# A graph layer's self-loop product: one small product per tile, or all of them at the start and a sum on VectorE

## The chip, the cores and the metric

The kernel runs on one core of a Trainium2 chip. Its time is device microseconds of one execution; given is the median of the runs, and less is better. A core has TensorE (matrix products into PSUM, eight banks of 128 x 512 float32), VectorE, ScalarE, GpSimd, and SyncE, which here only issues DMAs. Each engine works through its own program in order and waits for the others by semaphores.

## The reference

A graph of 3125 nodes and 103125 edges, sorted by destination, 128 features. First comes a relational layer with four bases and eight edge types, a self-loop product, a feed-forward product and two layer norms; then two attention layers (TransformerConv, two heads) and a last layer norm. The part that matters here:

```python
Hb = einsum('ni,bio->bno', h, V)              # four bases
m = sum_b w_comp[etype][:, b] * Hb[b][src]    # a message per edge
agg = segment_sum(m * norm, dst)
hn = relu(agg + h @ loop_w + bias)            # the self-loop product and its bias
y = hn @ ffn_w.T + ffn_b + h
y = layernorm(y) * ln_g + ln_b
x1 = layernorm(h + y)
```

Here h is the input x. All arithmetic is float32.

## The kernel before, in words

The 3125 nodes are 25 tiles of 125. For each tile of destination nodes the message stage gathers up to 64 edges per node by indirect DMA, builds for pairs of nodes a one-hot matrix of the sources' low digits (`low_onehot`) and a matrix of the edge weights by high digit and basis (`high_weights`), and multiplies them on TensorE (`pair_products`, L857). ScalarE copies the results out of PSUM (`evacuate`, L962). TensorE multiplies them with the rows of x (`sums`, L869: 25 products for each of the two halves of a tile), and ScalarE copies the result out as `aggT` (L981). The same matrices give edge counts, whose logarithm becomes a bias of 3125 columns per node for the attention layers (L972, L880, L989, L755); SyncE stores these in four pieces per tile (L639). A step of GpSimd, `coefs` (L574 to L577), makes the weights of a later tile's edges per basis.

The work is pipelined over steps. In the step t of the loop, w = t - 3 is the tile whose pairs are multiplied, u = t - 4 the tile whose sums are completed and activated, z = t - 5 the tile whose norms are finished. `pipeline_loop` writes the first and the last steps out and runs the others in a hardware loop, two per turn. The order within a step is written out by hand for each engine.

What becomes of one tile u within its step:
- TensorE multiplies the loop weights with the tile's turned features (`loopw`, `xt`, L935) and the four basis matrices with aggT (L937), all accumulated in one PSUM region `acc`. The middle piece of the next tile's first-half sums follows (`sums(w, 0, 1)`, nine products), then a wait for `h_ok` and `x_t_ok`, then the ffn product (L945), and then the last piece of these sums.
- ScalarE, between the first and the second half of its `counts_out`, applies Relu with the loop bias to acc and writes hT (L1041), and behind it copies the turned x1 of tile z over that tile's part of xT (L1043).
- VectorE adds the row x + ffn_b to the ffn product's result at the beginning of the next step (`first`, L769), and takes its moments. Its step consists mainly of `build_hot` (L734, L736, L739; eight per tile, four of them for the next tile and standing last in the step) and of `slot_kinds` before the last of these.

xT [128, 3125] holds the turned features. In the step of tile w = 0 TensorE turns all of x in groups of four tiles (`turn_inputs`, seven groups, two PSUM banks in turn), and ScalarE copies each group into xT (`turned_out`). Later each tile's part is overwritten with the turned x1, which the attention layers read. As the loop product needs the old features at an address that a register gives, ScalarE copies them first into the small tile `xT_tile` (L1002).

Of the kernel before, what the change touches and what calls it, by code (L numbers as in the profile page):

```python
# [71 lines left out]
def is_int(t):  # L72
    return isinstance(t, int)
# [116 lines left out]
def turn_inputs(nc, pe, m, turned_ps, turned_ok, at=0):  # L190

    x, eye, ps = m["x"], m["eye"], m["ps"][at:at + 2]
    pe.wait_ge(m["x_in"], 16)
    for n, (g, k) in enumerate(TURNS):
        if n >= 2:
            pe.wait_ge(turned_ok, n - 1)
        for i in range(k):
            last = nc.tensor.transpose(ps[n % 2][0:128, i * R:(i + 1) * R], x[:, g + i, :], eye[0:R, 0:R])
        last.then_inc(turned_ps, 1)


def turn_ffn(nc, pe, m, turned_ps, to):
# [256 lines left out]
def message(nc, a, m):  # L459
# [5 lines left out]
    with ctx:  # L465
        def sb(name, shape, dt):
            return ctx.enter_context(nc.sbuf_tensor(name, shape, dt))

        def sem(name):
            return ctx.enter_context(nc.semaphore(name))  # L470

        x, xT, eye, ones, iota, ids, ps = (m[k] for k in ("x", "xT", "eye", "ones", "iota", "ids", "ps"))
        V_b, comp, firsts, loopw, lcol = m["V"], m["comp"], m["firsts"], m["loop_w"], m["loop_bias_col"]
        gain, shift, ffnT, ffnb = m["ln_g"], m["ln_b"], m["ffnT"], m["ffn_b_rows"]
        SPLIT = 64
        SIDE = (SPLIT, R - SPLIT)
# [20 lines left out]
        CT = sb("countsT", [R, T, R], BF16)  # L497
        eye16 = sb("eye16", [128, 128], BF16)
        aggT = sb("aggT", [D, BASES, R], F32)
        xt = sb("xT_tile", [128, R], F32)  # L500
        lns = [sb(f"ln{i}", [R, RUN * R], F32) for i in range(2)]
        bias = [sb(f"bias{i}", [128, RUN * R], F32) for i in range(2)]
        tiny = sb("tiny", [128, 1], F32)
# [15 lines left out]
        psC = psM[:, :].bitcast(BF16).rearrange("p (h n) -> p h n", n=128)  # L519
        acc, psY, psX = psM[:, 256:256 + R], psM[0:R, 0:D], psM[:, 128:128 + R]  # L520
        (const, s2, slot_ok, gps, codes_ok, codes_ps, codesT_ok, hot, built, pairs_ok, evac_ok, agg_ok, aggT_ok,
         ctA_ok, ctB_ok, c_ps, ln_ok, bias_ok, xt_ok, m_ps, h_ok, y_ps, y_ok, x_ok, x_ps, x_t_ok, asked1, rooted1,
         asked2, rooted2, nrm1, nrm2, lifted, s3, kinds_ok, blank_ok, turned_ps, turned_ok, first_v, first_ok, digits_ps, digitsT_ok) = (
            sem("m_" + n) for n in (
                "const", "s2", "slot_ok", "pool", "codes_ok", "codes_ps", "codesT_ok", "hot", "built",
                "pairs_ok", "evac_ok", "agg_ok", "aggT_ok", "ctA_ok", "ctB_ok", "c_ps", "ln_ok", "bias_ok", "xt_ok", "m_ps",
                "h_ok", "y_ps", "y_ok", "x_ok", "x_ps", "x_t_ok", "asked1", "rooted1", "asked2", "rooted2",
                "norms1", "norms2", "lifted", "s3", "kinds_ok", "blank_ok", "turned_ps", "turned_ok",
                "first_v", "first_ok", "digits_ps", "digitsT_ok"))
        row_ok, row_in = m["m_row_ok"], [m["row_in0"], m["row_in1"]]  # L530
        near_in, kind_in = [sem("slot_ends_in0"), sem("slot_ends_in1")], [sem("slot_kinds_in0"), sem("slot_kinds_in1")]
        out_ok = [sem("bias_out0"), sem("bias_out1")]
# [123 lines left out]
        def _(v):  # L656
# [52 lines left out]
            def first_coefs():  # L709

                then = Steps(v, first_v)
                to = codes[0]
                v.wait_ge(m["comp_in"], 16)
                v.wait_ge(kinds_ok, 1)
                for b in range(BASES - FIRST_ON_V, BASES):
                    c = comp[:, :].rearrange("p (r b) -> p b r", b=BASES)[:, b, :].unsqueeze(2).to_broadcast([128, RELS, SLOTS])
                    then(V.tensor_tensor(part_v[:, :, :], kinds[:, :, :], c, ALU.mult))
                    then(V.tensor_tensor(part_v[:, 0:4, :], part_v[:, 0:4, :], part_v[:, 4:8, :], ALU.add))
                    then(V.tensor_tensor(part_v[:, 0:2, :], part_v[:, 0:2, :], part_v[:, 2:4, :], ALU.add))
                    last = V.tensor_tensor(to[:, b, :, :], twice(part_v[:, 0, :]), twice(part_v[:, 1, :]), ALU.add)  # L720
                    if b < BASES - 1:
                        then(last)
                last.then_inc(first_ok, 1)
# [57 lines left out]
            def third(z, par):  # L781

                v.wait_ge(rooted2, z + 1)
                if not is_int(z) or z >= 2:
# [2 lines left out]
                V.tensor_scalar(xnew[par][:, :], yb[par][:, :], means[1][par][:, 0:1], roots[1][par][:, :],  # L787
                                ALU.subtract, ALU.mult).then_inc(x_ok, 1)

            def step(t, par):  # L790
                w, u, z = t - 3, t - 4, t - 5
                for k in range(UNITS):
                    if k == 0 and inside(z):
                        first(z, 1 - par)
                    if k == 2 and inside(z):
                        second(z, 1 - par)
                    if k == 4 and inside(z):
                        third(z, 1 - par)
                    if k == 4 and inside(u):
                        bias_row(u, 3)  # L800
                    if k == 1 and inside(t) and (not is_int(t) or t >= EARLY):
                        search(nc, v, m, t, par)
                    if k == 2 and is_int(t) and t == 1:
                        for s in range(EARLY):
                            search_row(s, s)
                    if k == 2 and inside(t - 1) and (not is_int(t) or t > EARLY):
                        search_row(t - 1, 1 - par)
                    if k == UNITS - 1 and inside(t - 1) and (not is_int(t) or t > 2):
                        slot_kinds(t - 1, 1 - par)
                    if k < UNITS - AHEAD and inside(w):  # L810
                        build_hot(w, 1 - par, k + AHEAD)
                    if k >= UNITS - AHEAD and inside(w + 1):
                        build_hot(w + 1, par, k + AHEAD - UNITS)
                    if k == 2 and inside(u):
                        bias_row(u, 0)
                    if k == 3 and inside(u):
                        bias_row(u, 1)
                        bias_row(u, 2)
                    if k == UNITS - 1 and is_int(t) and t <= 2 and inside(t - 1):
                        slot_kinds(t - 1, 1 - par)  # L820
                    if k == UNITS - 1 and is_int(t) and t == 1:
                        first_coefs()
            pipeline_loop(v, step, AFTER, LEAD)

        @block.tensor
        def _(pe):
# [61 lines left out]
            def step(t, par):  # L888
# [2 lines left out]
                    pair_products(w, 0)  # L891
                if w == 0:
                    pe.wait_ge(codesT_ok, 1)
                    turn_inputs(nc, pe, m, turned_ps, turned_ok, 6)
                    pe.wait_ge(turned_ok, len(TURNS))
                if inside(z):
                    pe.wait_ge(y_ok, z + 1)
                if u == 0:
# [31 lines left out]
                    nc.tensor.transpose(psX, xnew[1 - par][:, :], eye[0:R, 0:R]).then_inc(x_ps, 1)  # L930
                if inside(u):
                    read(u, 3)
                    pe.wait_ge(xt_ok, u + 1)
                    pe.wait_ge(aggT_ok, u * 2 + 2)
                    nc.tensor.matmul(acc, loopw[:, :], xt[:, :], start=True, stop=False)  # L935
                    for b in range(BASES):
                        last = nc.tensor.matmul(acc, V_b[:, b, :], aggT[:, b, :], start=False, stop=(b == BASES - 1))  # L937
                    last.then_inc(m_ps, 1)
                if inside(w):
                    sums(w, 0, 1)  # L940
# [10 lines left out]
        def _(act):  # L951
# [40 lines left out]
            def step(t, par):  # L992
# [3 lines left out]
                if inside(w):  # L996
                    evacuate(w, 0)
                if is_int(w) and w == 0:
                    turned_out(nc, act, m, turned_ps, turned_ok, 6)
                if inside(u):  # L1000
                    logs(u, 0)
                    nc.scalar.copy(xt[:, :], xT[:, bass.ds(u * R, R)]).then_inc(xt_ok, 1)  # L1002
                    logs(u, 1)
                    logs(u, 2)
                if inside(w + 1):
# [27 lines left out]
                if inside(z):  # L1033
                    act.wait_ge(x_ps, z + 1)
                if inside(u):
                    act.wait_ge(m_ps, u + 1)
                    if is_int(u) and u == 0:
                        act.wait_ge(m["w_in"], W_IN)
                    if not is_int(u) or u >= 1:
                        act.wait_ge(y_ps, u)  # L1040
                    nc.scalar.activation(hT[:, :], acc, ACT.Relu, bias=lcol[:, :]).then_inc(h_ok, 1)  # L1041
                if inside(z):
                    nc.scalar.copy(xT[:, bass.ds(z * R, R)], psX).then_inc(x_t_ok, 1)  # L1043
                if inside(w):
# [5 lines left out]
def message_any(nc, a, m):  # L1050
# [4 lines left out]
    with ctx:  # L1055
# [25 lines left out]
        names = ("e_in", "iota_ok", "dve", "at_ok", "settled", "g_in", "stored", "m_in", "summed", "xt_ok", "ln_ok", "bias_out")  # L1081
        z = {n: sem(n) for n in names}
        cw = widths()
        SUMS = BLOCKS + 2
# [35 lines left out]
        @block.scalar  # L1120
        def _(act):
            with act.Fori(0, T) as t:

                act.wait_ge(z["dve"], 1 + t * CHAIN)
                nc.scalar.copy(xt[:, :], xT[:, bass.ds(t * R, R)]).then_inc(z["xt_ok"], 1)
                act.wait_ge(z["summed"], (t + 1) * SUMS)
                for j in range(CH):
                    last = nc.scalar.activation(lns[:, CW * j:CW * j + cw[j]], ps[j][0:R, 0:cw[j]], ACT.Ln, bias=tiny[0:R, :])
                last.then_inc(z["ln_ok"], 1)

        @block.tensor
        def _(pe):
            pe.wait_ge(z["e_in"], 32)
            with pe.Fori(0, T) as t:

                pe.wait_ge(z["dve"], 1 + t * CHAIN)
                pe.wait_ge(z["xt_ok"], t + 1)
# [648 lines left out]
```

## Time and profile before

| what | value |
|---|---|
| median of 3 runs | 1972.24 us (1970.37 to 1975.23) |
| the profiled execution's own time | 1973.57 us |
| its span | 1971.7 us |
| TensorE busy | 1898.3 us, 96% |
| VectorE busy | 1448.8 us, 73% |
| ScalarE busy | 1281.9 us, 65% |
| GpSimd busy | 671.4 us, 34% |

The profile records one execution. An engine's busy time counts its own work, not waits, nor register and semaphore instructions. The span starts with the first recorded instruction; the execution's own time holds what lies around it as well. The message stage ends at about 1056 us, the two attention layers fill the rest. The message stage's profile is a repeating pattern with a period of one tile.

### The profile page before, as it was taken

What the parts mean: (1) busy time and instruction counts of PE and PEld (TensorE: products, weight loads), DVE (VectorE), ACT (ScalarE), POOL (GpSimd) and SP (SyncE); (2) the same over time, 40 slices, a digit from 0 to 9 for tenths busy, and PEclk for the clock granted to TensorE, in tenths of its full rate; (3) what the DMA queues carried; (4) which work ended last, traced back from release to release, by engine and by line L of the source; (5) the groups of instructions that cost most, each with busy time, mean ns of one, the idle gap of its engine ahead of it and who ended that gap; (6) DMA issues with size and microseconds to landing.
All of it is one profiled execution on the core that took longest, in us unless ns stands there. A gap on an engine that the chain in (4) does not pass through costs nothing. (4 is left out here: it accounts for less than half of the span.)

```text
span 1971.7 us, 53479 instructions
## 1 busy us (share of the span) xinstructions
PE 1898.3 (96%) x19165; PEld 1645.7 (83%) x19165; DVE 1448.8 (73%) x4127; ACT 1281.9 (65%) x2289; POOL 671.4 (34%) x802
## 2 busy tenths in 40 slices
PE   1899999999999999999998999999999999999998
PEld 1789999999999999999995788888887788888887
DVE  5888878887888788878744777676663777777775
ACT  0757766776677767776764666666665666666665
POOL 3676676667666765676400000000000000000000
PEclk9999999999999999999998999999999999999999
DMA  3012111211121111111103222222211233222230
GB/s 84 8 47 73 41 41 45 75 41 41 48 72 41 41 54 67 40 41 52 61 35 129 103 100 97 80 83 97 97 65 66 101 107 106 99 92 92 103 105 11
DMA packets 43019, 137.00 MB, mean 69 GB/s; under 512 B 9191, under 2 KB 24360, under 8 KB 36485
## 3 DMA queue, kind: packets, MB, share of 16 engines
q1 hardware_dynamic: 38484, 128.24, 18.1%
q0 software_dynamic: 4400, 6.80, 1.5%
q8 instruction: 104, 1.70, 0.4%
q14 instruction: 31, 0.25, 0.0%
HBM read 91.83 MB, written 43.20 MB: 68 GB/s over the span
## 5 line engine op out<-in xcount | busy, mean ns | idle before, releaser
L869 PE MATMUL ps<-matrixT,x_rows 125*128 125x256 f32 (+1 forms) x2500 | 563.5, 377 | 0.1
L869 PEld LDWEIGHTS ps<-matrixT,x_rows 125*128 125x128 f32 x2500 | 461.4, 190 | 48.4 <-issue 0.2
L1729 DVE CUSTOM_DVE_ANT_0 scores_l<-ps,bias_rows_l 125x500 f32<-125x500 f32 (+1 forms) x700 | 390.0, 619 | 29.9 <-issue 28.9
L962 ACT COPY matrixT<-ps 125x500 f32<-125x500 f32 (+2 forms) x800 | 381.6, 653 | 38.9 <-PE ps L857 38.9
L857 PE MATMUL ps<-high_weights,low_onehot 64*125 64x125 f32 x6300 | 363.9, 273 | 8.6 <-DVE high_weights L739 8.6
L857 PEld LDWEIGHTS ps<-high_weights,low_onehot 64*125 64x125 f32 x6300 | 354.1, 187 | 21.6 <-issue 15.8
L1630 ACT ACTIVATE scores_l<-scores_l,neg_max_l 125x1500 f32<-125x1500 f32 x200 | 317.3, 1600 | 7.2 <-DVE neg_max_l L1750 7.2
L1518 PEld LDWEIGHTS ps<-weightsT_l,values_l 125*64 125x64 f32 x5000 | 267.9, 136 | 36.4 <-issue 34.1
L1559 PE MATMUL ps<-eye,scores_l 125*125 125x125 f32 x2500 | 295.2, 275 | 0.0
L1559 PEld LDWEIGHTS ps<-eye,scores_l 125*125 125x125 f32 x2500 | 281.1, 189 | 10.1 <-issue 9.5
L1541 PE MATMUL ps<-kT_l,q_tile_l 64*125 64x500 f32 (+1 forms) x1400 | 287.2, 547 | 1.7 <-issue 1.6
L1518 PE MATMUL ps<-weightsT_l,values_l 125*64 125x125 f32 x5000 | 279.7, 270 | 1.6 <-ACT hT L1658 1.6
L1638 ACT COPY weightsT_l<-ps 125x500 f32<-125x500 f32 x400 | 220.6, 578 | 91.8 <-PE ps L1559 86.9
L736 DVE TENSOR_TENSOR low_onehot<-own_low,digitsT 128x1000 f32<-128x1000 f32 x200 | 280.2, 1401 | 0.0
L1737 DVE COPY weightsT_l<-ps 125x500 f32<-125x500 f32 x200 | 135.0, 677 | 159.6 <-PE ps L1559 159.4
L1541 PEld LDWEIGHTS ps<-kT_l,q_tile_l 64*125 64x125 f32 x1400 | 144.0, 183 | 112.4 <-issue 77.5
L739 DVE TENSOR_TENSOR high_weights<-high_weights,edge_weightsT 128x800 f32<-128x800 f32 x200 | 222.4, 1112 | 0.0
L574 POOL TENSOR_TENSOR coef_parts<-kinds,comp 128x512 f32<-128x512 f32 x97 | 119.4, 1231 | 234.9 <-DVE digits L703 230.6
L989 ACT ACTIVATE ln<-ps,tiny 125x1000 f32<-125x1000 bf16 x100 | 95.5, 955 | 128.2 <-DVE bias L755 87.7
L1472 POOL COPY q_tile_l<-qT_l 128x125 f32 (+1 forms) x52 | 15.3, 293 | 436.7 <-PE ps L1541 403.0
L972 ACT CAST countsT<-matrixT 125x512 bf16<-125x512 f32 (+1 forms) x200 | 162.0, 949 | 0.0
L734 DVE TENSOR_TENSOR high_weights<-iota,digitsT 128x200 f32<-128x200 f32 x200 | 79.2, 396 | 99.6 <-PE ps L857 93.0
(152 smaller groups left out, 1605.1 us busy)
## 6 DMA issues: line engine op xcount, KB each, us to landing
bias_rows_l<-bias SPq DMA_DIRECT2D x50, 1562.5 KB, 6.5
bias<-bias SPq DMA_DIRECT2D x75, 500.0 KB
x_rows<-in_x SPq DMA_DIRECT2D x1, 1562.5 KB
bias<-bias SPq DMA_DIRECT2D x25, 62.5 KB
x<-x_rows SPq DMA_DIRECT2D x25, 62.5 KB
x_rows_l<-x SPq DMA_DIRECT2D x25, 62.5 KB
out<-rows_l SPq DMA_DIRECT2D x25, 62.5 KB
dst_int<-in_dst SPq DMA_DIRECT2D x1, 402.8 KB
```

What stands on the lines that cost most here:

```text
L736: V.tensor_tensor(L[:, at, 0:p, :], own_low[:, :].unsqueeze(1).to_broadcast([128, p, R]), digitsT[par][:, 0, to].unsqueeze(2).to_broadcast ...
L739: V.tensor_tensor(Hw[:, at, 0:p, 0:BASES * T].rearrange("p n (h b) -> p n h b", b=BASES), hots.unsqueeze(3).to_broadcast([128, p, T, BASES ...
L857: last = nc.tensor.matmul(psP[2 * bank + q][0:R, 128 * (i % 4):128 * (i % 4) + COLS], L[own, at, i % GROUP, :], Hw[own, at, i % GROUP, 0:C ...
L869: last = nc.tensor.matmul(psG[:, BASES * SPLIT * side:BASES * (SPLIT * side + SIDE[side])], x[:, h, :], MT[side][:, 0:SIDE[side], BASES * ...
L962: last = nc.scalar.copy(MT[side][:, at:at + 2 * c - 1:2, 0:COLS], psP[2 * (g % 3) + q][0:R, :].rearrange("p (i c) -> p i c", c=128)[:, 0:c ...
L972: nc.scalar.copy(CT[:, lo:hi, SPLIT * side:SPLIT * side + SIDE[side]], MT[side][:, 0:SIDE[side], BASES * T + lo:BASES * T + hi].rearrange( ...
L1518: last = nc.tensor.matmul(psO[HD * hd:HD * (hd + 1), 0:R], vals[:, 4 * c + b, hd, :], weights, start=(c == 0 and b == 0), stop=(c == CH - ...
L1541: nc.tensor.matmul(score_bank(t, k)[0:R, 0:cw[j]], q_now[par][own, :], kT[own, CW * j:CW * j + cw[j]], start=True, stop=True).then_inc(z[" ...
L1559: last = nc.tensor.transpose(turn_bank(i)[0:R, at:at + R], S[up][:, hd, n * R:(n + 1) * R], eye[0:R, 0:R])
L1630: nc.scalar.activation(part, part, ACT.Exp, bias=neg[par][:, hd:hd + 1], accum_out=sums[par][:, hd, n // 2:n // 2 + 1]).then_inc(z["exp_ok ...
L1638: nc.scalar.copy(PT[i][:, 0:cw[c]], turn_bank(i)[0:R, 0:cw[c]]).then_inc(z["pa_ok"], 1)
L1729: V.tensor_tensor_reduce(S[par][:, hd, lo:hi], score_bank(t, HEADS * n + hd)[0:R, 0:cw[j]], bias[par][0:R, lo:hi], 1.0, FLOOR, ALU.add, AL ...
```

## The change

The loop products of all nodes are made at the start. In the step of w = 0, `loop_terms` takes the place of `turn_inputs`: between the turnings of the seven groups, TensorE multiplies the loop weights with each turned group (up to 500 columns) into the same PSUM bank. ScalarE (`loop_terms_out`) copies the turned group into xT, and after the product writes product plus loop bias over the same part of xT. A bank is used again when the second evacuation of its group is done. Per tile, TensorE's loop product and ScalarE's copy into `xT_tile` are gone. A new step `add_loop` on VectorE, last in its step, adds the tile's part of xT to acc and writes `m_hT_sum`. ScalarE's Relu reads this tile, without a bias, and waits for `loop_in` in place of `m_ps`. (A name of a semaphore in the path for irregular graphs, which these inputs don't take, changes as well.)

```diff
+def loop_terms(nc, pe, m, turned_ps, turned_ok, loop_ps, loop_ok, at):
+
+    x, xT, eye, ps = m["x"], m["xT"], m["eye"], m["ps"][at:at + 2]
+    pe.wait_ge(m["x_in"], 16)
+    pe.wait_ge(m["w_in"], W_IN)
+    for n in range(len(TURNS) + 1):
+        if n < len(TURNS):
+            g, k = TURNS[n]
+            if n >= 2:
+                pe.wait_ge(loop_ok, n - 1)
+            for i in range(k):
+                last = nc.tensor.transpose(ps[n % 2][0:128, i * R:(i + 1) * R], x[:, g + i, :], eye[0:R, 0:R])
+            last.then_inc(turned_ps, 1)
+        if n >= 1:
+            g, k = TURNS[n - 1]
+            pe.wait_ge(turned_ok, n)
+            nc.tensor.matmul(ps[(n - 1) % 2][:, 0:k * R], m["loop_w"][:, :], xT[:, g * R:(g + k) * R], start=True, stop=True).then_inc(loop_ps, 1)
+
+
+def loop_terms_out(nc, act, m, turned_ps, turned_ok, loop_ps, loop_ok, at):
+
+    xT, ps = m["xT"], m["ps"][at:at + 2]
+    act.wait_ge(m["w_in"], W_IN)
+    for n in range(len(TURNS) + 1):
+        if n < len(TURNS):
+            g, k = TURNS[n]
+            act.wait_ge(turned_ps, n + 1)
+            nc.scalar.copy(xT[:, g * R:(g + k) * R], ps[n % 2][:, 0:k * R]).then_inc(turned_ok, 1)
+        if n >= 1:
+            g, k = TURNS[n - 1]
+            act.wait_ge(loop_ps, n)
+            nc.scalar.activation(xT[:, g * R:(g + k) * R], ps[(n - 1) % 2][:, 0:k * R], ACT.Identity,
+                                 bias=m["loop_bias_col"][:, :]).then_inc(loop_ok, 1)
...
-        xt = sb("xT_tile", [128, R], F32)
+        hsum = sb("m_hT_sum", [D, R], F32)
...
+            def add_loop(u):
+
+                v.wait_ge(m_ps, u + 1)
+                if not is_int(u) or u >= 1:
+                    v.wait_ge(h_ok, u)
+                V.tensor_tensor(hsum[:, :], acc, xT[:, bass.ds(u * R, R)], ALU.add).then_inc(loop_in, 1)
...
+                if inside(u):
+                    add_loop(u)
             pipeline_loop(v, step, AFTER, LEAD)
...
-                    turn_inputs(nc, pe, m, turned_ps, turned_ok, 6)
-                    pe.wait_ge(turned_ok, len(TURNS))
+                    loop_terms(nc, pe, m, turned_ps, turned_ok, loop_ps, loop_ok, 6)
+                    pe.wait_ge(loop_ok, len(TURNS))
...
-                    pe.wait_ge(xt_ok, u + 1)
                     pe.wait_ge(aggT_ok, u * 2 + 2)
-                    nc.tensor.matmul(acc, loopw[:, :], xt[:, :], start=True, stop=False)
                     for b in range(BASES):
-                        last = nc.tensor.matmul(acc, V_b[:, b, :], aggT[:, b, :], start=False, stop=(b == BASES - 1))
+                        last = nc.tensor.matmul(acc, V_b[:, b, :], aggT[:, b, :], start=(b == 0), stop=(b == BASES - 1))
                     last.then_inc(m_ps, 1)
...
-                    turned_out(nc, act, m, turned_ps, turned_ok, 6)
+                    loop_terms_out(nc, act, m, turned_ps, turned_ok, loop_ps, loop_ok, 6)
                 if inside(u):
                     logs(u, 0)
-                    nc.scalar.copy(xt[:, :], xT[:, bass.ds(u * R, R)]).then_inc(xt_ok, 1)
...
-                    act.wait_ge(m_ps, u + 1)
-                    if is_int(u) and u == 0:
-                        act.wait_ge(m["w_in"], W_IN)
+                    act.wait_ge(loop_in, u + 1)
                     if not is_int(u) or u >= 1:
                         act.wait_ge(y_ps, u)
-                    nc.scalar.activation(hT[:, :], acc, ACT.Relu, bias=lcol[:, :]).then_inc(h_ok, 1)
+                    nc.scalar.activation(hT[:, :], hsum[:, :], ACT.Relu).then_inc(h_ok, 1)
```

## Rows read from the trace of the kernel before

**Rows 1.** Table of stretches: busy us of each engine (instructions), TensorE's clock, DMA share, GB/s.
```profile
200.00:400.00 200.00, 199.79 (x2001) 183.56 (x2000) 162.37 (x334) 139.87 (x268) 129.45 (x136) 1.00 0.14 50
```
**Rows 2.** Timeline of TensorE, one tile: start us, us, engine, line, operation [idle before].
```profile
875.37 0.38 PE L945 MATMUL ps<-ffnT,m_hT 128*125 128x128 f32 x2
...
909.66 0.39 PE L935 MATMUL ps<-xT_tile,loop_w 128*128 128x125 f32 x2
909.88 1.06 PE L937 MATMUL ps<-aggT,V 128*128 128x125 f32 x8
...
914.66 0.38 PE L945 MATMUL ps<-ffnT,m_hT 128*125 128x128 f32 x2
...
918.00 2.23 PE L857 MATMUL ps<-high_weights,low_onehot 64*125 64x125 f32 x36
```
**Rows 3.** Timeline of ScalarE, evacuations of one tile's pairs, then the tile of rows 2.
```profile
506.62 7.46 ACT L962 COPY matrixT<-ps 125x500 f32<-125x500 f32 x16 [0.34 <-PE ps L857]
...
911.02 0.37 ACT L1041 ACTIVATE m_hT<-ps,loop_bias_col 128x125 f32<-128x125 f32 x1 [0.70 <-issue]
911.29 0.26 ACT L1043 COPY xT<-ps 128x125 f32 x1
911.43 3.10 ACT L972 CAST countsT<-matrixT 125x488 bf16<-125x488 f32 x4
918.11 0.37 ACT L981 COPY aggT<-ps 128x256 f32<-128x256 f32 x1 [3.58 <-PE ps L869]
```
**Rows 4.** Timeline of VectorE, the tile of rows 2.
```profile
900.63 0.37 DVE L734 TENSOR_TENSOR high_weights<-iota,digitsT 128x200 f32<-128x200 f32 x1 [0.18 <-PE ps L857]
900.91 1.19 DVE L736 TENSOR_TENSOR low_onehot<-own_low,digitsT 128x1000 f32<-128x1000 f32 x1
...
910.31 2.06 DVE L736 TENSOR_TENSOR low_onehot<-own_low,digitsT 128x1000 f32<-128x1000 f32 x1
912.29 1.51 DVE L739 TENSOR_TENSOR high_weights<-high_weights,edge_weightsT 128x800 f32<-128x800 f32 x1
915.15 0.29 DVE L769 TENSOR_TENSOR m_y_rows<-ps,x_raised 125x128 f32<-125x128 f32 x1 [1.35 <-PE ps L945]
```
**Rows 5.** Timeline, two handovers between engines: VectorE to ScalarE, ScalarE to TensorE.
```profile
539.50 1.18 DVE L755 SCALAR_TENSOR_TENSOR bias<-ln 125x1000 f32<-125x1000 f32 x1
540.78 1.09 ACT L989 ACTIVATE ln<-ps,tiny 125x1000 f32<-125x1000 bf16 x1 [3.50 <-DVE bias L755]
...
1050.35 0.25 ACT L1043 COPY xT<-ps 128x125 f32<-128x125 f32 x1
1050.75 0.45 PE L945 MATMUL ps<-ffnT,m_hT 128*125 128x128 f32 x2 [0.75 <-ACT xT L1043]
```
**Rows 6.** Timeline of VectorE, the first and last of three tiles with a shorter gap.
```profile
246.25 0.29 DVE L769 TENSOR_TENSOR m_y_rows<-ps,x_raised 125x128 f32<-125x128 f32 x1 [0.84 <-PE ps L945]
...
522.02 0.29 DVE L769 TENSOR_TENSOR m_y_rows<-ps,x_raised 125x128 f32<-125x128 f32 x1 [1.02 <-PE ps L945]
```
**Rows 7.** Timeline of VectorE, the first build behind the y rows.
```profile
526.92 0.72 DVE L734 TENSOR_TENSOR high_weights<-iota,digitsT 128x200 f32<-128x200 f32 x1 [3.88 <-PE ps L857]
```
**Rows 8.** Timeline of three engines in the step of the first tile.
```profile
54.35 1.07 PE L198 MATMUL ps<-eye,x_rows 125*128 125x125 f32 x8
55.77 1.22 ACT L213 COPY xT<-ps 128x500 f32<-128x500 f32 x2
...
76.21 0.74 ACT L1023 COPY edge_weightsT<-ps 64x252 f32<-64x252 f32 x2 [0.29 <-PE ps L840]
76.98 0.37 DVE L734 TENSOR_TENSOR high_weights<-iota,digitsT 128x200 f32<-128x200 f32 x1 [5.22 <-ACT edge_weightsT L1023]
```
**Rows 9.** Timeline, a product of 500 columns and its evacuation.
```profile
1062.95 1.00 PE L1499 MATMUL ps<-xT,Wk 128*128 128x500 f32 x2
1063.99 0.68 ACT L1614 ACTIVATE kT_l<-ps,bk 128x500 f32<-128x500 f32 x1 [0.16 <-PE ps L1499]
```
**Rows 10.** Table of short stretches, TensorE alone: busy us, granted clock, DMA share, GB/s.
```profile
72.00:74.00 2.00, 2.00 (x20) 0.50 0.00 0
```

More of the change, by code:

```diff
@@ L472, in message @@
         x, xT, eye, ones, iota, ids, ps = (m[k] for k in ("x", "xT", "eye", "ones", "iota", "ids", "ps"))
-        V_b, comp, firsts, loopw, lcol = m["V"], m["comp"], m["firsts"], m["loop_w"], m["loop_bias_col"]
+        V_b, comp, firsts = m["V"], m["comp"], m["firsts"]
         gain, shift, ffnT, ffnb = m["ln_g"], m["ln_b"], m["ffnT"], m["ffn_b_rows"]
@@ L521, in message @@
         (const, s2, slot_ok, gps, codes_ok, codes_ps, codesT_ok, hot, built, pairs_ok, evac_ok, agg_ok, aggT_ok,
-         ctA_ok, ctB_ok, c_ps, ln_ok, bias_ok, xt_ok, m_ps, h_ok, y_ps, y_ok, x_ok, x_ps, x_t_ok, asked1, rooted1,
-         asked2, rooted2, nrm1, nrm2, lifted, s3, kinds_ok, blank_ok, turned_ps, turned_ok, first_v, first_ok, digits_ps, digitsT_ok) = (
+         ctA_ok, ctB_ok, c_ps, ln_ok, bias_ok, loop_in, m_ps, h_ok, y_ps, y_ok, x_ok, x_ps, x_t_ok, asked1, rooted1,
+         asked2, rooted2, nrm1, nrm2, lifted, s3, kinds_ok, blank_ok, turned_ps, turned_ok, first_v, first_ok, loop_ps, loop_ok, digits_ps, digitsT_ok) = (
             sem("m_" + n) for n in (
                 "const", "s2", "slot_ok", "pool", "codes_ok", "codes_ps", "codesT_ok", "hot", "built",
-                "pairs_ok", "evac_ok", "agg_ok", "aggT_ok", "ctA_ok", "ctB_ok", "c_ps", "ln_ok", "bias_ok", "xt_ok", "m_ps",
+                "pairs_ok", "evac_ok", "agg_ok", "aggT_ok", "ctA_ok", "ctB_ok", "c_ps", "ln_ok", "bias_ok", "loop_in", "m_ps",
                 "h_ok", "y_ps", "y_ok", "x_ok", "x_ps", "x_t_ok", "asked1", "rooted1", "asked2", "rooted2",
                 "norms1", "norms2", "lifted", "s3", "kinds_ok", "blank_ok", "turned_ps", "turned_ok",
-                "first_v", "first_ok", "digits_ps", "digitsT_ok"))
+                "first_v", "first_ok", "loop_ps", "loop_ok", "digits_ps", "digitsT_ok"))
         row_ok, row_in = m["m_row_ok"], [m["row_in0"], m["row_in1"]]
@@ L1080, in message_any @@
         spare = sb("spare", [128, 1], F32)
-        names = ("e_in", "iota_ok", "dve", "at_ok", "settled", "g_in", "stored", "m_in", "summed", "xt_ok", "ln_ok", "bias_out")
+        names = ("e_in", "iota_ok", "dve", "at_ok", "settled", "g_in", "stored", "m_in", "summed", "loop_in", "ln_ok", "bias_out")
         z = {n: sem(n) for n in names}
@@ L1124, in _ @@
                 act.wait_ge(z["dve"], 1 + t * CHAIN)
-                nc.scalar.copy(xt[:, :], xT[:, bass.ds(t * R, R)]).then_inc(z["xt_ok"], 1)
+                nc.scalar.copy(xt[:, :], xT[:, bass.ds(t * R, R)]).then_inc(z["loop_in"], 1)
                 act.wait_ge(z["summed"], (t + 1) * SUMS)
@@ L1136, in _ @@
                 pe.wait_ge(z["dve"], 1 + t * CHAIN)
-                pe.wait_ge(z["xt_ok"], t + 1)
+                pe.wait_ge(z["loop_in"], t + 1)
                 nc.tensor.matmul(ps[CH][0:R, 0:D], xt[:, :], loopw[:, :], start=True, stop=False)
```

## The prediction

> **What bounds the kernel now.** I read the table of stretches first. In the steady part of the message stage TensorE is busy for 199.79 of 200 us [rows 1]: what leaves TensorE is worth its own length, as long as nothing new makes it wait. The change touches only this stage and its first step; the two attention layers behind it only start earlier or later.
>
> Then I read the timeline of one tile. On TensorE the loop product (L935) starts at 909.66, the four products of the bases (L937) at 909.88, nine sums follow, and the product with the ffn (L945) starts at 914.66; the next tile's pairs start at 918.00. The tile before has its L945 at 875.37, 39.29 us earlier [rows 2].
>
> The question is how late the activated sum h may be. ScalarE makes it from 911.02 to 911.39 and copies the turned x1 behind it, done at 911.55 [rows 3]: 3.1 us before TensorE takes both at 914.66. VectorE has no part in this chain now. It starts its builds for the next tile at 900.63, released by TensorE's own pairs, and runs without a gap to the end of the last build, 912.29 + 1.51 = 913.80. It then idles 1.35 us until L945 gives it the rows of y [rows 4]. So VectorE is free only 0.86 us before L945 starts. That number decides the change.
>
> **The change, part by part.**
> *Removed per tile:* one TensorE product, 909.66 to 909.88, 0.22 us [rows 2], on the bounding engine: 25 x 0.22 = 5.5 us if nothing waits. ScalarE's copy into xT_tile goes too; ScalarE has idle time (3.58 us ahead of L981) [rows 3], so this is worth 0.
>
> *Added per tile, a hop through VectorE.* add_loop stands last in VectorE's step, behind the last build. Its own waits (base products done at 910.94, h of the tile before) are long over. The nearest row for a 125-column sum of a PSUM and an SBUF tile is L769, 0.29 us; in a run of instructions the next begins some 0.08 us before the end of the one before [rows 4]. From F, the end of the last build:
> - the sum ends at F + 0.21;
> - ScalarE begins 0.10 us later (L755 ends at 540.68, L989 begins at 540.78) [rows 5]: F + 0.31;
> - Relu 0.37 us, and the copy of the turned x1 ends 0.16 us after it [rows 3]: F + 0.84;
> - TensorE starts 0.15 us after the copy (1050.60 to 1050.75) [rows 5]: F + 0.99.
>
> With F = L945 - 0.86 the product starts 0.13 us later than before in the normal tile. A product that had to wait lasts 0.45 in place of 0.38 us [rows 2, 5], another 0.07. So such a tile becomes 0.20 us longer in place of 0.22 shorter: TensorE stalls for some 0.4 us in each. It doesn't heal by itself: VectorE's builds are released by TensorE's pairs, so F moves with TensorE and each tile pays again. This holds for tiles 0 to 21; behind tile 22 no slots are prepared any more and VectorE is early. Three of the 22 tiles have VectorE later still, the first with a gap of 0.84 us and the last with 1.02 in place of 1.35 [rows 6], after a longer wait for a bias store; the three together pay 1.5 us more. Total 22 x 0.20 + 1.5 = 5.9 us. The last three tiles: twice -0.22, and in the last one, where the chain is bare, +0.29 + 0.10 - 0.22; together -0.3.
>
> Bounds of the hop: if the Relu without its bias operand lasts only as long as the copy, 0.26 [rows 3], each tile is 0.11 shorter, -2.4 in all. If the sum is stretched as the one-hot builds are while GpSimd works (2.06 in place of 1.19) [rows 4], it takes 0.50, and each tile is 0.21 longer, +4.6. I take 0.29 and 0.37, the rows of the like operations.
>
> The rows show 0.37 us for the activation with its bias and 0.26 for the copy without [rows 3]. The Trainium skill (ScalarE: Activation LUTs, What ACT_TABLE_LOAD costs) gives about 93 ns for each pointer operand of an ACTIVATE; the trace agrees. By that rule alone the sum would be 2.0 us less, unless the default bias is a pointer as well. Another page speaks against the change: the Trainium skill's VectorE: DVE Perf Modes (The TRN2 errata) gives ScalarE 52 cycles, some 0.04 us, more from SBUF than from PSUM, and the Relu now reads SBUF; by that alone the sum would be 1.0 us more. I leave both out.
>
> *What queues behind.* On VectorE the y rows follow, and then a wait of 3.88 us for pairs [rows 7], so nothing there is late. On ScalarE the four casts of 3.10 us that followed at 911.43 now begin near 914.5 and end near 917.7; L981 behind them is wanted at 918.11 [rows 3]. Covered, with 0.4 us to spare; without that cover the evacuations would be late by the difference.
>
> *The first step (paid once).* Seven products of up to 500 columns and seven evacuations join the turning. Before, the turning starts at 54.35 and its first copy ends at 56.38 [rows 8]. There are two banks, and a bank is free only when its second evacuation is done, so this becomes a ring: four transposes 0.5 us [rows 8], product to evacuation 1.04 us (1062.95 to 1063.99), evacuation 0.68 [rows 9], way back 0.15: 2.37 us a group. The first evacuation ends at 56.53 + 1.04 + 0.68 = 58.25, five rings later, the last of them short, it is 69.7, and the pairs behind start at some 70.3. Most of this is hidden, because those pairs stood waiting for VectorE: it idles 5.22 us until 76.98, so its last build was ready at 71.76 [rows 8], and the turning doesn't hold it up. All pairs then find their input; ScalarE needs 7.46 us for the 16 copies out of their banks [rows 3], from about 71.5, and reaches the edge weights at 79.1 in place of 76.21 [rows 8]. VectorE waits for these, and all that follows is 2.9 us later. Lower bound 2.0, if TensorE's end and not ScalarE's decides; the upper bound is the third rival.
>
> **The sum.** 2.9 + 5.9 - 0.3 = +8.5 us on the profiled execution's own 1973.57 us (span 1971.7 and 1.9 around it): 1982.1. The median of the runs is 1.3 lower than that execution, so I forecast 1980.7 us, 0.4% slower. What a measurement of this kernel can tell from no change is about 0.3%, 5.9 us.
>
> **Rivals.**
> 1. *VectorE is in time and the gain stays* (the other side). From F the hop may last 0.64 us; beyond that TensorE waits. For it: with GpSimd quiet the one-hot part of the last build takes 1.19 and not 2.06 us [rows 4], which alone would do. Against: 1.35 is the gap in nearly every tile. Then 2.9 - 5.5 = -2.6: 1969.6, or 1967 if the start costs nothing. Chance 0.12.
> 2. *Half stalls.* The hop takes 0.2 us less than I sum (the Relu's bound and an overlap), a tile comes out even, and the start alone shows: 1972.24 + 2.9 + 1.2 = 1976.3. Chance 0.22.
> 3. *The clock drops in the ring.* From 72 to 74 us the granted clock is 0.50 (the 1.2 GHz level), after TensorE had stood waiting for builds [rows 10]. In the ring it works some 60% of the time. At that level products and transposes take twice as long, 1.3 us more a ring, 6.5 in all on top of the forecast: 1987. Against: no single wait in the ring is above 1 us. Chance 0.11. By the Trainium skill (TensorE: Matmul & The Clock Gate, Part 1) throttled is the default and activity releases it; the trace agrees.
> 4. *A longer hop, or late stores in most tiles:* 0.3 us more a tile: 1987. Chance 0.08.
>
> The forecast (1977.5 to 1984) has 0.47, of which a little lies below the 0.3% mark at 1978.1. Faster by over 0.3%, under 1966.3, needs rival 1 and no cost at the start: 0.04. Within 0.3%: the rest of 1, all of 2, and 0.03 of the forecast, 0.33. Slower by over 0.3%: 0.63. Range 1973 to 1989.
>
> **What would show it.** L945's distances are 39.4 to 39.6 us in place of 39.29; TensorE waits some 0.4 us ahead of the ffn product in tiles 0 to 21, released by ScalarE; the Relu waits some 3 us a tile for VectorE; neither happens in tile 22. The turning with its products lasts to about 70, the pairs behind it have no waits for VectorE, and the edge weights come at 79.1. If the distances are 39.07, I am wrong on the hop; if the edge weights come after 82, on the start; if the attention layers change length, on what the change touches.

## The result and the profile after

The changed kernel takes 1979.44 us (median of 12 runs), the kernel before 1974.45 in 12 runs beside it: ratio 1.0025, 95% interval 1.0016 to 1.0034, 4.9 us slower. The forecast was 1980.7 us and +8.5 us; the interval allows 3.2 to 6.7. The direction is clear of the interval, and its size lies just under the 0.3% that I had given as the mark: of my three classes it is the middle one (0.33) and not the likeliest (0.63).

First the page of the changed kernel: its span is 4.9 us longer than that of before, and TensorE's busy time is no smaller.
```profile
span 1976.6 us, 53446 instructions
PE 1900.5 (96%) x19129; PEld 1640.0 (83%) x19129; DVE 1453.0 (74%) x4152; ACT 1279.9 (65%) x2271; POOL 670.2 (34%) x802
```
Next the timeline of one tile of the changed kernel, all engines that take part (start us, us, engine, line, operation, idle before). It answers to [rows 2], [rows 3] and [rows 4].
```profile
881.29 0.46 PE L987 MATMUL ps<-ffnT,m_hT 128*125 128x128 f32 x2
...
915.64 1.06 PE L979 MATMUL ps<-aggT,V 128*128 128x125 f32 x8
918.29 1.51 DVE L774 TENSOR_TENSOR high_weights<-high_weights,edge_weightsT 128x800 f32<-128x800 f32 x1
919.72 0.28 DVE L830 TENSOR_TENSOR m_hT_sum<-ps,xT 128x125 f32<-128x125 f32 x1
920.08 0.31 ACT L1080 ACTIVATE m_hT<-m_hT_sum 128x125 f32<-128x125 f32 x1 [3.79 <-issue]
920.29 0.24 ACT L1082 COPY xT<-ps 128x125 f32 x1
920.68 0.45 PE L987 MATMUL ps<-ffnT,m_hT 128*125 128x128 f32 x2
920.97 3.19 PE L913 MATMUL ps<-matrixT,x_rows 125*128 125x256 f32 x14
921.24 0.29 DVE L804 TENSOR_TENSOR m_y_rows<-ps,x_raised 125x128 f32<-125x128 f32 x1 [1.25 <-PE ps L987]
924.20 0.38 ACT L1023 COPY aggT<-ps 128x256 f32<-128x256 f32 x1 [0.66 <-PE ps L913]
```
The base products are over at 916.70, but the sum starts only at 919.72, when VectorE's last build (to 919.80) lets it. From there to the ffn product it takes 0.88 us. The distance to the tile before is 39.39 us, where it was 39.29 [rows 2]. ScalarE waited 3.79 us ahead of the Relu, and L981's counterpart, L1023, still has 0.66 us to spare.

The step of the first tile of the changed kernel, which answers to [rows 8]:
```profile
56.79 1.10 PE L218 MATMUL ps<-xT,loop_w 128*128 128x500 f32 x2 [1.05 <-ACT xT L229]
58.67 0.65 PE L213 MATMUL ps<-eye,x_rows 125*128 125x125 f32 x4 [0.77 <-ACT xT L233]
59.15 1.01 PE L218 MATMUL ps<-xT,loop_w 128*128 128x500 f32 x2
60.93 0.65 PE L213 MATMUL ps<-eye,x_rows 125*128 125x125 f32 x4 [0.77 <-ACT xT L233]
...
70.11 7.06 PE L901 MATMUL ps<-high_weights,low_onehot 64*125 64x125 f32 x124
78.47 0.82 ACT L1064 COPY edge_weightsT<-ps 64x252 f32<-64x252 f32 x2
79.33 0.37 DVE L769 TENSOR_TENSOR high_weights<-iota,digitsT 128x200 f32<-128x200 f32 x1 [7.84 <-ACT edge_weightsT L1064]
```
Each group costs 60.93 - 58.67 = 2.26 us, and every turning waits 0.77 us for the second evacuation: the ring. The edge weights come at 78.47 in place of 76.21, VectorE at 79.33 in place of 76.98.

One thing more in this trace, in the table of short stretches, TensorE alone (busy us, granted clock, DMA share, GB/s), where before shows a clock of 1.00:
```profile
114.00:116.00 2.00, 2.00 (x26) 0.64 1.01 402
116.00:118.00 2.00, 2.00 (x22) 0.50 0.48 105
```
Ahead of it TensorE waits twice for a logarithm, 2.09 and 1.99 us. The pairs behind these take 8.68 us in place of 7.14. The change isn't the cause. A later trace of the unchanged kernel, c0 below, has the same spell in the same pairs (its table of short stretches, then its timeline):
```profile
112.00:114.00 2.00, 2.00 (x22) 0.50 0.51 133
110.09 8.67 PE L857 MATMUL ps<-high_weights,low_onehot 64*125 64x125 f32 x124
```

The bookkeeping by starts of the ffn product: the first tile's at 131.24 in place of 127.56, +3.7 us, of which some 1.5 are this spell; from tile 0 to tile 22, 868.28 in place of 866.00, +2.3; from there to the last, at 1056.52 in place of 1050.75, -0.2; behind it, 920.1 in place of 921.0, -0.9 in the attention layers that nothing in the change touches. Together +4.9.

### The profile page after: what moved, and what is told of

Same layout as the page of the kernel before. It is cut to its first block and busy times, and to the rows that moved or that the text cites. A ratio compares the mean times of both kernels' runs of the same rounds, so it can differ in the third digit from the quotient of the medians.

```text
span 1976.6 us, 53446 instructions
## 1 busy us (share of the span) xinstructions
PE 1900.5 (96%) x19129; PEld 1640.0 (83%) x19129; DVE 1453.0 (74%) x4152; ACT 1279.9 (65%) x2271; POOL 670.2 (34%) x802
```

## The experiments

There were three series, each with its own runs of before: 1986.6 us in the first, 1984.1 in the second, 1974.1 in the third. The first two ran on one chip, the third on another. The first of these chips differs from the second, and from that of the result, in one place of each tile, so a ratio is read only within its series. A table of medians over tiles 2 to 20, taken from the timelines (A: ffn product to the turning of the edge weights; B: from there to the first sum, the pairs; C: to the base products; D: to the next ffn product; E: in the first step, from the first edge weights to the second, which leaves out when the program got going):

| kernel, series | A | B | C | D | E | tile 0 to 22 | ratio to before (95%) |
|---|---|---|---|---|---|---|---|
| before, the prediction | 22.67 | 7.53 | 4.32 | 4.78 | 34.0 | 866.0 | |
| changed, the result | 22.73 | 7.53 | 4.09 | 5.04 | 36.6 | 868.3 | 1.0025 (1.0016 to 1.0034) |
| e1, series 1 | 22.67 | 8.23 | 4.09 | 4.78 | 40.6 | 874.6 | 1.0030 (1.0019 to 1.0042) |
| e2, series 1 | 22.67 | 8.10 | 4.32 | 4.78 | 40.5 | 876.8 | 1.0034 (1.0021 to 1.0047) |
| e3, series 1 | 22.74 | 8.08 | 4.10 | 5.02 | 32.4 | 878.0 | 1.0004 (0.9995 to 1.0013) |
| e4, series 1 | 22.77 | 8.21 | 4.10 | 5.30 | 40.5 | 886.4 | 1.0094 (1.0080 to 1.0109) |
| c0 = before, series 2 | 22.67 | 8.08 | 4.32 | 4.78 | 32.4 | 874.7 | |
| c1 = changed, series 2 | 22.74 | 8.08 | 4.09 | 5.01 | 44.2 | 878.0 | 1.0054 (1.0037 to 1.0071) |
| e5, series 2 | 22.73 | 8.10 | 4.10 | 5.02 | 32.4 | 877.6 | 1.0018 (1.0009 to 1.0026) |
| e6, series 2 | 22.72 | 8.25 | 4.09 | 4.78 | 32.7 | 874.4 | 1.0001 (0.9991 to 1.0012) |
| c2 = changed, series 3 | 22.74 | 7.53 | 4.10 | 5.03 | 38.2 | 868.8 | 1.0036 (1.0027 to 1.0046) |
| e7, series 3 | 22.74 | 7.58 | 4.10 | 4.78 | 32.4 | 862.3 | 0.9992 (0.9981 to 1.0003) |
| e8, series 3 | 22.67 | 7.58 | 4.10 | 4.78 | 33.5 | 863.5 | 0.9991 (0.9982 to 0.9999) |

**e1, the sum ahead of VectorE's last build**
```diff
+                    if k == UNITS - 1 and inside(u):
+                        add_loop(u)
                     if k >= UNITS - AHEAD and inside(w + 1):
                         build_hot(w + 1, par, k + AHEAD - UNITS)
...
-                if inside(u):
-                    add_loop(u)
```


> The changed kernel, with add_loop moved ahead of the last build of VectorE's step (behind slot_kinds); nothing else. Theory (TensorE waits for a hop that starts only when VectorE has done its last build): VectorE is at the sum some 0.9 us before the base products are done, so h is ready about 1 us behind them and 2.5 us before TensorE needs it. No wait ahead of the ffn product in any tile, distances from one ffn product to the next 39.07 us in place of 39.39, and the kernel 22 x 0.32 = 7 us faster than the changed one, so 2 us faster than the kernel before (ratio 0.999). Rival (the tile's length comes from elsewhere, the stores or VectorE's own load): distances stay at 39.3 to 39.4 and the time stays 5 us above before; VectorE's last build, now 1.2 us later, could even make the next pairs wait.

Measured: 1.0030, where 0.999 was expected; the time is that of the rival. The mechanism still behaved as the theory has it: D is 4.78 in place of 5.02 in e3. The time did not follow, because the expectation leant on the first chip for two sums that this one changes, the start (E is 40.6) and B, which is 0.13 us longer than in e2. From tile 0 to 22 it takes 874.6 us against 878.0 in e3, which has the late place: 3.4 us less, half of the 7 expected. e5 and e6 differ in the place alone and settle it.

**e2, the start alone**
```diff
-                    turn_inputs(nc, pe, m, turned_ps, turned_ok, 6)
-                    pe.wait_ge(turned_ok, len(TURNS))
+                    loop_terms(nc, pe, m, turned_ps, turned_ok, loop_ps, loop_ok, 6)
+                    pe.wait_ge(loop_ok, len(TURNS))
...
-                    turned_out(nc, act, m, turned_ps, turned_ok, 6)
+                    loop_terms_out(nc, act, m, turned_ps, turned_ok, loop_ps, loop_ok, 6)
```


> The kernel before, with the changed kernel's first step: the seven products and seven evacuations in the ring, and the tiles as before with their own loop product (it then multiplies what the start has written, which makes other values and leaves the work per tile as it was). Theory: the start alone costs 2.4 us up to the edge weights and, if TensorE's clock drops again behind the waits for the logarithms near 115 us, 1.2 us more: 2.4 to 3.6 us slower than before (ratio 1.0012 to 1.0018), tiles at 39.29 us. Rival (the ring is hidden by the wait for VectorE's builds, and the whole loss is in the tiles): within 0.5 us of before.

Measured: 1.0034, 6.7 us (4.2 to 9.3), twice what was expected and far from the rival. The ring itself takes 2.26 us a group, as above. It is behind it that TensorE stands still. The timeline of e1, which has the same first step, TensorE and then one line of ScalarE; the granted clock is 1.00 up to 82 us:
```profile
71.49 5.51 PE L901 MATMUL ps<-high_weights,low_onehot 64*125 64x125 f32 x96
77.23 0.78 PE L901 MATMUL ps<-high_weights,low_onehot 64*125 64x125 f32 x9 [0.23 <-ACT matrixT L1004]
78.19 0.51 PE L901 MATMUL ps<-high_weights,low_onehot 64*125 64x125 f32 x5 [0.18 <-issue]
79.63 0.39 PE L901 MATMUL ps<-high_weights,low_onehot 64*125 64x125 f32 x2 [0.93 <-issue]
80.78 1.09 PE L901 MATMUL ps<-high_weights,low_onehot 64*125 64x125 f32 x12 [0.76 <-ACT matrixT L1004]
79.67 1.06 ACT L1004 COPY matrixT<-ps 125x500 f32<-125x500 f32 x2 [2.58 <-remote]
```
96 instructions run without a stop, and the rest of the group takes 4.6 us where 1.6 are its length. Half of the waits are put down to nothing ("issue"), half to ScalarE's copies; and ScalarE itself stands still for 2.58 us, released by nothing that this core's profile shows ("remote"). So two engines pause together. e1, e2 and e4 all show it. Before, these pairs are stretched by the waits for VectorE's builds. What the engines stand still for I can't say from the profile. It means that E of these three, 40.5, is the ring, this pause and, at the very end, a spell of low clock (0.50 from 82 to 84 us in e1).

**e3, the tiles alone** (the seven products and their evacuations are left out, so the sum adds the turned features themselves)
```diff
-                    loop_terms(nc, pe, m, turned_ps, turned_ok, loop_ps, loop_ok, 6)
-                    pe.wait_ge(loop_ok, len(TURNS))
+                    turn_inputs(nc, pe, m, turned_ps, turned_ok, 6)
+                    pe.wait_ge(turned_ok, len(TURNS))
```


> The changed kernel, with the turning of the kernel before: the seven products and their evacuations are left out (so the sum adds the turned features themselves), the tiles as changed. Theory: only the tiles' part is left, 22 x 0.10 us and the end's -0.3, 1.5 to 2.5 us slower than before (ratio 1.001), tiles at 39.39 us, the edge weights at 76.2 us, no low clock near 115 us. Rival (the start is the whole loss): same time as before; other rival (the tiles' part is a consequence of the start's delay): tiles at 39.1.

Measured: 1.0004 (-1.0 to +2.6 us). D is 5.02, C is 4.10, E is back at 32.4. The interval holds both the theory's +2 and nothing, so it rules out a gain of more than 1 us and doesn't tell the size of the loss. But the segments are those of the changed kernel, without its start: the tile's part is not a consequence of the start's delay.

**e4, the sum twice, at its late place**
```diff
+                V.tensor_tensor(again[:, :], acc, xT[:, bass.ds(u * R, R)], ALU.add)
                 V.tensor_tensor(hsum[:, :], acc, xT[:, bass.ds(u * R, R)], ALU.add).then_inc(loop_in, 1)
```


> The changed kernel, with the sum made twice in a row by VectorE, the first into a tile that nobody reads. Theory: the hop is 0.20 us longer (0.28 less the overlap of 0.08), and as TensorE already waits for it in tiles 0 to 21, each is 0.20 us longer: distances 39.59, 4.4 us slower than the changed kernel, 9 to 10 us slower than before (ratio 1.005). Rival (the hop is hidden, as the ffn product has room): no change against the changed kernel, 1.0025.

Measured: 1.0094, 18.7 us over before, twice what was expected; some 8 of it is the start (E is 40.5, in c0 32.4). The timeline of a tile in e4:
```profile
616.70 1.06 PE L981 MATMUL ps<-aggT,V 128*128 128x125 f32 x8
620.84 0.27 DVE L831 TENSOR_TENSOR sum_again<-ps,xT 128x125 f32<-128x125 f32 x1
621.04 0.27 DVE L832 TENSOR_TENSOR m_hT_sum<-ps,xT 128x125 f32<-128x125 f32 x1
621.39 0.31 ACT L1082 ACTIVATE m_hT<-m_hT_sum 128x125 f32<-128x125 f32 x1 [4.05 <-issue]
622.00 0.45 PE L989 MATMUL ps<-ffnT,m_hT 128*125 128x128 f32 x2 [0.35 <-ACT xT L1084]
```
0.20 us more on VectorE is 0.28 more in D and 0.4 in the whole tile (8.3 us over the tiles of e3). The rival, a hidden hop, is out: TensorE is released by this chain, and the addition came out in full. The 0.08 us more in D, and the 0.13 in B (8.21 against 8.08 in e3), I can't account for.

**c1, the changed kernel again, and c0, the kernel before, for its profile**

> The changed kernel once more, as it is, to stand beside the others on one chip. On the chip of the second study the kernel before takes 12 us more, 0.55 us in each tile in the pairs behind the edge weights, and the start costs more than on the first. Theory (tiles 2.3 us, start 3.7 us on the first chip): ratio to before 1.0025 on a chip like the first. If this is a chip like the second, where TensorE's queue stands still in the pairs behind the turning without anything in the profile to wait for, the start costs 6 to 9 us and the ratio is 1.004 to 1.006. Rival (the small difference was chance): 1.000 to 1.001.

> The kernel before, for its profile on the chip of this call. Theory: segments of a tile of 22.67 us (ffn product to edge weights), 7.5 us on a chip like the first or 8.1 on one like the second (edge weights to sums), 4.32 and 4.78 us. Rival: the other chip's segments differ in the second place too, by the changed kernels themselves.

Measured: 1.0054, within what was expected of this chip, though this profile shows another cause than the expected pause. c0 has the segments of before but for B, 8.08 in place of 7.53, so the other chip's 0.55 us a tile has nothing to do with the change. It also has a start 1.6 us shorter than that of before (E 32.4 in place of 34.0). The last pair products ahead of the edge weights, before and then c0:
```profile
71.82 3.31 PE L857 MATMUL ps<-high_weights,low_onehot 64*125 64x125 f32 x28 [0.96 <-DVE high_weights L739]
71.95 1.79 PE L857 MATMUL ps<-high_weights,low_onehot 64*125 64x125 f32 x28 [1.69 <-DVE high_weights L739]
```
The kernel before had the 0.50 clock of [rows 10] here, and c0 has 1.00.

c1 shows my third rival. The table of short stretches of c1, TensorE alone:
```profile
60.00:64.00 4.00, 3.23 (x8) 0.50 0.00 0
64.00:68.00 4.00, 3.23 (x8) 0.50 0.00 0
```
and its timeline:
```profile
59.84 1.80 PE L218 MATMUL ps<-xT,loop_w 128*128 128x500 f32 x2
62.41 1.10 PE L213 MATMUL ps<-eye,x_rows 125*128 125x125 f32 x4 [0.77 <-ACT xT L233]
63.30 1.88 PE L218 MATMUL ps<-xT,loop_w 128*128 128x500 f32 x2
65.95 1.10 PE L213 MATMUL ps<-eye,x_rows 125*128 125x125 f32 x4 [0.77 <-ACT xT L233]
```
A product of 500 columns takes 1.88 us in place of 1.01 and a group 3.54 in place of 2.26; the edge weights come at 87.25, against 74.70 in c0. The clock stays at the 1.2 GHz level until 80 us, in the pairs behind. Against the changed kernel of the result E is 44.2 in place of 36.6, so the low clock cost 7.6 us, if nothing else differs between the two. In c2 the ring ran at full clock, and only the pairs behind it were slow (0.76 and 0.82 from 68 to 76 us, E 38.2).

**e5, the opened ring** (the products into the pairs' six banks, free at this point)
```diff
+    pe.wait_ge(evac_ok, UNITS)
...
             if n >= 2:
-                pe.wait_ge(loop_ok, n - 1)
+                pe.wait_ge(turned_ok, n - 1)
...
-            nc.tensor.matmul(ps[(n - 1) % 2][:, 0:k * R], m["loop_w"][:, :], xT[:, g * R:(g + k) * R], start=True, stop=True).then_inc(loop_ps, 1)
+            if n >= 7:
+                pe.wait_ge(loop_ok, n - 6)
+            nc.tensor.matmul(own[(n - 1) % 6][:, 0:k * R], m["loop_w"][:, :], xT[:, g * R:(g + k) * R], start=True, stop=True).then_inc(loop_ps, 1)
```


> The changed kernel, with the products of the start written to the six banks of the pairs, free then, in place of the bank that still holds the turned group: the ring is opened, and a turning waits only for the copy of the group two before it. Tiles as changed. Theory: ScalarE sets the pace with 0.5 + 0.6 us per group, so the start ends near 64 us in place of 69.9, before VectorE's last build at 71.5, and the edge weights come at 76.2 to 76.6 us as before the change. The kernel is then 3 to 4 us faster than the changed one of this call (more where TensorE's queue stood still behind the ring), and 1 to 2 us slower than before. Rival (the start's cost isn't the ring but the seven products and evacuations as such): no more than 1 us faster than the changed one.

Measured: 1.0018 against the changed kernel's 1.0054 in the same series, 7 us less. The start in e5:
```profile
58.81 0.59 PE L214 MATMUL ps<-eye,x_rows 125*128 125x125 f32 x4
59.24 1.01 PE L221 MATMUL ps<-xT,loop_w 128*128 128x500 f32 x2
60.08 0.59 PE L214 MATMUL ps<-eye,x_rows 125*128 125x125 f32 x4
...
66.38 7.38 PE L904 MATMUL ps<-high_weights,low_onehot 64*125 64x125 f32 x124
74.73 0.82 ACT L1067 COPY edge_weightsT<-ps 64x252 f32<-64x252 f32 x2
```
A group takes 1.27 us, no group waits for the one before it, the clock is 1.00 up to the edge weights, and E is 32.4, that of c0. The same products and evacuations cost nothing here: the start's price was the ring, with what came behind it. In all four profiles with the opened ring E is 32.4 to 33.5, in the six with the closed one 36.6 to 44.2. How much of the 7 us is the ring's waits, how much the pause behind it and how much the clock, this pair doesn't tell; where neither of the last two showed (the result), the ring's waits were 36.6 - 32.4 = 4.2 us, if a start at full clock takes the 32.4 us of c0, e3 and e7 on that chip too. What is left over before, 3.6 us (1.8 to 5.2), is the tiles in the main: 877.6 against 874.7 us from tile 0 to 22.

**e6, opened ring and early sum**

> Both: the opened ring at the start, and the sum ahead of VectorE's last build. Theory: 0.32 us a tile less than the spread start alone (no wait ahead of the ffn product, segment from the base products to the ffn product 4.78 us in place of 5.03), 7 us in all; 5 us faster than before (ratio 0.9975). Rival (from the second study, where the early sum did take the wait away and the kernel was still 0.3% slower than before: what TensorE gains is lost in the pairs behind the edge weights, which took 0.13 us more in each tile): half of it, 3 to 4 us less than the spread start alone.

Measured: 1.0001, 3.4 us less than e5 by the two ratios, and 3.1 less from tile 0 to 22. D is 4.78, 0.24 less than in e5, but B is 0.15 us longer. The rival's number held, and it is not faster than before on this chip.

**e7, as e6 with the sum twice, and e8, e6 again, on a chip like the first**

> Opened ring and early sum as in e6, with the sum made twice in a row, the first into a tile that nobody reads. At the early place the sum has some 2.9 us before the ffn product, so by the theory of the hop the second one costs nothing on that side: the segment from the base products to the ffn product stays at 4.78 us (at the late place the same edit lengthened it by 0.28). Theory of the next limit (with the early sum VectorE's chain from the pairs over the bias rows to the last logarithm, which ends at 19.30 us behind the start of the pairs where TensorE wants it at 19.34, has no room left): up to 0.2 us a tile shows ahead of the edge weights, 2 to 4 us over e6 of this call. Rival (VectorE still has room, as it waits 3.88 us for pairs in each tile): same time as e6 within 1 us.

> The kernel of e6 again, beside the others of this call. On a chip where the pairs behind the edge weights take 7.5 us, theory: tiles 39.1 us, 5 us faster than before (ratio 0.9975). On one where they take 8.1, as in e6: no difference from before, since 0.2 us a tile goes back to these pairs and the chain ahead of them.

> The changed kernel again, beside the others of this call: on a chip like the first 1.0025 and tiles of 39.4 us, on one like the second 1.0054, tiles of 39.93 and a start that ends in queue stalls of TensorE.

Measured: e8 0.9991, e7 0.9992, c2 1.0036, where 0.9975, some 0.999 to 0.9995 and 1.0025 were expected. At the early place the second sum costs nothing (e7 equals e8), where at the late place it cost 8.3 us: one edit, two places, and the difference is whether VectorE's last build stands ahead of it. The timeline of a tile in e7:
```profile
631.54 1.06 PE L984 MATMUL ps<-aggT,V 128*128 128x125 f32 x8
632.75 0.29 DVE L834 TENSOR_TENSOR sum_again<-ps,xT 128x125 f32<-128x125 f32 x1 [0.75 <-PE ps L984]
632.95 0.28 DVE L835 TENSOR_TENSOR m_hT_sum<-ps,xT 128x125 f32<-128x125 f32 x1
633.32 0.31 ACT L1085 ACTIVATE m_hT<-m_hT_sum 128x125 f32<-128x125 f32 x1 [1.12 <-issue]
636.32 0.38 PE L992 MATMUL ps<-ffnT,m_hT 128*125 128x128 f32 x2
```
The Relu is done at 633.63, 2.7 us before it is needed. e8 is 0.45% faster than the changed kernel of its series and beats the kernel before by 1.8 us, at the edge of its interval, where 5 were expected. Six of its 22 tiles take 39.07 or 39.08 us, as the theory says, but seven take 39.11 to 39.14, and five take 39.5 to 39.9, with A at 22.81 in the mean against 22.67 in the median. In e8 and e6 the last logarithm ends 19.3 us behind the start of the pairs, against 19.05 before, and TensorE wants it at 19.3. So part of the product's 0.22 us is now lost to VectorE's chain ahead of the edge weights. That this chain is what takes it back is argued from these ends; e7's expected 2 to 4 us on top did not come.

## Why the prediction was right

*The bound and the deciding gap.* Right. TensorE had no idle time, VectorE's last build ended 0.86 us before the ffn product, and a hop of more than 0.64 us from there had to turn a saving into a wait. The hop was 0.88 us. e4 and e7 show the place: the same second sum costs 8.3 us behind the last build and nothing ahead of it. e3 has the late place's D without the start.

*The hop's size.* Forecast 0.99, measured 0.88 (F at 919.80, product at 920.68). The sum (0.28), the handovers (0.02 us off at most) and the 0.07 us of a product that had to wait (0.29 us from the ffn product to the next sums, before 0.22) were as taken. The Relu was 0.31 us and not 0.37, between the two bounds of the rows, 0.26 and 0.37. I had left out the rule on pointer operands of the Trainium skill (ScalarE: Activation LUTs, What ACT_TABLE_LOAD costs), by which it would be some 0.09 less; 0.06 less was seen, with the input in SBUF in place of PSUM as well. The two rules that I left out come together to 0.05 less and were closer to the measurement than my row was; no run separates them.

*The sum over the tiles.* Forecast 5.9, measured 2.3 us: the mis-sized term. The ordinary tile is 0.10 us longer and not 0.20, which is the 0.11 of the hop; over 22 tiles that is 2.2 us of the difference. The late stores cost three tiles 1.3 us more than the others, near the 1.5 forecast, but I had set these on top of a kernel before that has uneven tiles of its own: 39.85, 39.50 and five of 39.45, 1.6 us in all over 39.29. Tile by tile, a late store moved from one waiting place into another and was not added.

*The start.* Forecast 2.9 us to the edge weights, measured 2.3 (2.6 without the chip's entry), with the ring's 2.26 us for 2.37, the pairs at 70.11 for 70.3 and no wait for builds behind. Part of this agreement is luck. The trace that I started from had the low clock of [rows 10] in the very pairs ahead of the edge weights, and I took its 76.21 us as the kernel's own. c0, the same kernel at full clock, is 1.6 us quicker there. Against that, and if the chips are alike here, the ring costs 4.2 us and not 2.6. Behind the edge weights the result then lost 1.5 us to a low clock that I had not priced, and that is not the change's work either, as c0 has it too.

And I gave the clock in the ring a chance of 0.11 and a price of 6.5 us. It came in full in one of three profiles of the changed kernel, at 7.6 us. The mean granted clock of a run points the same way: it is 0.990 or 0.991 in 5 of the 46 runs of kernels with the closed ring, and 0.994 or more in all 130 other runs of the three series. So the chance was about right for one execution, but what happens in one of nine doesn't move a median, and as a rival of the forecast it was given too much. That "no single wait in the ring is above 1 us" spoke against it was wrong: in c1 the groups ahead of the fall had waits of 0.77 us.

*The number.* The ratio shows +4.9 us where +8.5 was forecast. The median of 1979.44 us lies nearer to the 1980.7 forecast than that, because the kernel before was 2.2 us slower in the 12 runs than in the 3 that I had counted from: luck.

*The rivals.* VectorE in time: no, in any run with the late place. A hidden or even tile: no. The case with the highest chance, tiles a little longer and a start that is paid, was the right one in its mechanism. With +4.9 us its size fell between it and half stalls, since both the tiles and the start were smaller than summed.

## What to carry to other kernels

Before moving work off the busiest engine, look when the engine that is to take it gets free, against when the result is wanted: the idle share of VectorE was 27%, and what counted was 0.86 us at one place. A sum of 0.28 us cost TensorE more than the product of 0.22 us that it replaced, and with the sum one build earlier the wait ahead of the ffn product was gone, though part of that gain was lost again elsewhere in the tile. And when a prologue gains a second evacuation per PSUM bank, count the banks before the work: by E the same seven products cost 4 to 12 us on two banks and 0 to 1 on eight. Last, before one trace serves as the base of a sum of a few us, look at its granted clock stretch by stretch: two profiles of the same kernel differed by 1.6 us in the start alone.

## What the runs showed of the hardware

- In the ring TensorE is busy 2.46 of every 4 us at full rate. In one run (after) the clock stayed at the 2.4 GHz level there, in another run of the same program (c1) it went to the 1.2 GHz level at about 60 us and stayed until 80. A group then took 3.54 us in place of 2.26.
- Short spells at the lower level come and go between runs of one kernel: from 70 to 76 us in before and not in c0, from 110 to 116 us in c0 and not in before. Each made the pairs in it 1.5 us longer. In e6 TensorE waits 2.03 and 2.00 us for the logarithms near 110 us, about as in the changed kernel, and the clock stays up.
- The chips differ in the pairs behind the edge weights, in the kernel before too: 0.55 us a tile, 9 to 10 of the 10 to 12 us between the chips. On one kind of chip ScalarE's first evacuation starts 1.72 us behind the turning of the edge weights and the rest follow without a gap. On the other it either starts at about 2.27, or ScalarE pauses for 0.48 us behind the second evacuation. e1, e4 and e6, in which B is some 0.13 us longer still, mostly have the second form. The cause stays open.
- Behind the ring TensorE and ScalarE stood still together, some 3 us in all, in the three kernels of the first series that have the ring, and in none of the others. A pause of the same look, 1.89 us in ScalarE and again "remote", comes in the pairs of the next tile in e2, c1 and e6. In e2 these pairs take 9.35 us, where before takes 7.14. e6 has the opened ring, so it isn't the ring alone that brings it on. All of these ran on one chip. Open as well.
